# Graph attention, linear attention and an expert FFN on one core: the fills between gathers are replaced by a wait of each gather for the one before

## The reference, cut to what matters

```python
xn = layernorm(x)
f  = xn @ W_n                                  # (N, 8 heads, 32)
el, er = f . attn_l, f . attn_r                # (N, 8, 4) each
e  = ((el[src] + er[dst] + edge16 . attn_m) * edge4).sum(4) / 3.0
e  = where(e > 0, e, 0.2 * e)                  # (E, 8)
a  = softmax of e over the edges of each dst
gnn = segment_sum(f[src] * a, dst)             # (N, 256)
mix = linear attention over all nodes, then layernorm * gamma
x  = x + gnn + mix
x  = x + sum over 8 experts of w_e * FFN_e(layernorm(x))
```

## Time and profile before

| | us |
|---|---|
| median of 2 runs | 3389.78 (3389.61 to 3389.95) |
| the profiled execution | 3383.94 |
| its span in the trace | 3382.3 |
| GpSimd busy | 2077.2 |
| VectorE busy | 2641.9 |
| TensorE busy | 2979.6 |

### The profile page before, as it was taken

One profiled execution on the slowest core, in us unless ns is written; L12 is line 12 of the kernel. 1 busy time (PEld: TensorE's weight loads), 2 busy tenths in 40 slices (PEclk: granted clock), 3 DMA queues, 4 the chain that ended last, 5 costly groups with the idle time before them and its releaser, 6 DMA issues. The chain is left out here.

```text
span 3382.3 us, 76670 instructions
## 1 busy us (share of the span) xinstructions
PE 2979.6 (88%) x21350; PEld 2402.1 (71%) x21351; DVE 2641.9 (78%) x4924; ACT 1699.5 (50%) x5754; POOL 2077.2 (61%) x3347
## 2 busy tenths in 40 slices
PE   7995648889898888998988889888859999999999
PEld 4564537777676767776766677676648888888899
DVE  4574548889888888988988889888857777777786
ACT  4651216556555555665655566555543433333343
POOL 2888878888888888888888888888500000000000
PEclk9997769999999999999999999999879999999999
DMA  7567876666666666666666666666331000100000
GB/s 270 182 209 242 304 239 198 183 181 193 194 187 184 184 195 191 187 187 196 193 182 182 202 184 191 183 194 188 98 98 42 20 20 23 37 20 17 17 21 10
DMA packets 285469, 509.70 MB, mean 151 GB/s; under 512 B 84049, under 2 KB 186870, under 8 KB 277508
## 3 DMA queue, kind: packets, MB, share of 16 engines
q0 software_dynamic: 86032, 287.41, 29.8%
q1 hardware_dynamic: 198900, 220.45, 20.6%
q10 hardware_dynamic: 384, 0.00, 0.0%
HBM read 415.38 MB, written 92.29 MB: 150 GB/s over the span
## 5 line engine op out<-in xcount | busy, mean ns | idle before, releaser
L978 POOL DMA_INDIRECT gat<-scratch_table,idx x1376 | 1332.0, 968 | 231.6 <-issue 226.8
L1337 PE MATMUL ps_s<-msg,oh 128*128 128x272 f32 x4000 | 1055.9, 414 | 41.4 <-DVE msg L1183 26.3
L1337 PEld LDWEIGHTS ps_s<-msg,oh 128*128 128x128 f32 x4000 | 758.5, 197 | 198.1 <-ACT tmp L1044 42.1
L1053 ACT ACTIVATE acc<-acc,sc 128x33 f32<-128x33 f32 x2000 | 458.8, 339 | 230.4 <-DVE acc L1171 230.4
L1580 POOL DMA_DIRECT2D out<-y x13 | 9.8, 756 | 899.6 <-DVE y L1794 899.6
L1183 DVE TENSOR_TENSOR msg<-gat,ps_m 128x2048 f32<-128x2048 f32 x250 | 559.2, 2276 | 0.0
L1627 ACT ACTIVATE h<-ps_h,fsh,fsc 128x512 f32<-128x512 f32 (+1 forms) x416 | 290.8, 750 | 508.9 <-PE ps_h L1840 508.9
L1044 ACT ACTIVATE tmp<-ps_s,sc 128x33 f32<-128x33 f32 x2000 | 384.4, 304 | 17.2
L140 POOL MEMSET rest_e<- 128x192 f32 x1376 | 388.3, 282 | 0.7
L1033 ACT CAST oh<-ps_o 128x1024 f32<-128x1024 bf16 x250 | 259.1, 1037 | 143.4 <-PE ps_o L1277 122.4
L1670 DVE CAST h_hi<-h 128x1024 fp32r<-128x1024 f32 (+1 forms) x208 | 137.2, 660 | 201.7 <-ACT h L1627 201.5
(11 more groups left out here) (217 smaller groups left out, 5406.1 us busy)
## 6 DMA issues: line engine op xcount, KB each, us to landing
d16r<-scratch_dst SPq DMA_DIRECT2D x250, 256.0 KB
scratch_ahead<-stage SPq DMA_DIRECT2D x30, 1152.0 KB, 4.8
gat<-scratch_ahead POOLq DMA_DIRECT2D x30, 1152.0 KB
scratch_acc<-acc SPq DMA_DIRECT2D x250, 136.0 KB
gat<-scratch_table,idx POOLq DMA_INDIRECT x1376
edge<-in_edge SPq DMA_DIRECT2D x250, 88.0 KB
scratch_table<-trow POOLq DMA_DIRECT2D x49, 144.0 KB, 4.1
xin<-in_x SPq DMA_DIRECT2D x49, 128.0 KB, 4.4
```

The costliest lines, as they stand in the source:

```text
L978: pool.indirect_dma_start(out=gat[:, s, c, :], out_offset=None, in_=scr["table_rows"], in_offset=bass.IndirectOffsetOnAxis(ap=idx[:, g * C ...
L1053: act.mul(acc[:, new, cols], acc[:, old, cols], sc[:, j, 0, h:h + 1]).then_inc(scaled, 1)
L1337: last = pe.matmul(ps_s[j][:, 0:SUMS], oh[:, s, j, c, :], msg[:, 2 * (s % 2) + j, c, :], start=(c == 0), stop=(c == C - 1), skip_group_che ...
```

## The change

The class `Rests` and its two scratch tiles go, and with them 1616 fills. The class `Turns` comes in its place. Every gather now raises a semaphore (`engine_sem`) when GpSimd has finished it, apart from the semaphore that the transfer itself raises when the rows have landed, and every gather but the first of a stage waits for the semaphore of the gather before it. The semaphores are the same two as before (`made`, `rested`). The direct loads of groups gathered ahead neither wait nor are waited for.

```diff
-class Rests:
-
-
-    def __init__(self, tile, rested, n):
-        self.tile, self.rested, self.n = tile, rested, n
-
-    def after(self, pool, c):
-        if c % REST_AFTER != REST_AFTER - 1:
-            return
-        for _ in range(RESTS):
-            if self.n:
-                pool.wait_ge(self.rested, self.n)
-            pool.memset(self.tile[:, :], 0.0).then_inc(self.rested, 1)
-            self.n += 1
+class Turns:
+
+
+    def __init__(self, done, n):
+        self.done, self.n = done, n
+
+    def before(self, pool):
+        if self.n:
+            pool.wait_ge(self.done, self.n)
+
+    def begun(self):
+        self.n += 1
+        return self.done
...
                 for c in range(C):
+                    turns.before(pool)
                     pool.indirect_dma_start(
-                        out=stage[:, i % 2, c, :], out_offset=None, in_=scr["table_rows"],
+                        engine_sem=turns.begun(), out=stage[:, i % 2, c, :], out_offset=None, in_=scr["table_rows"],
                         in_offset=bass.IndirectOffsetOnAxis(ap=pidx[:, i * C + c:i * C + c + 1], axis=0),
                     ).then_inc(staged[i % 2], 16)
-                    rests.after(pool, c)
...
             def gather(g, c):
                 s = g % GSLOTS
+                turns.before(pool)
                 pool.indirect_dma_start(
-                    out=gat[:, s, c, :], out_offset=None, in_=scr["table_rows"],
+                    engine_sem=turns.begun(), out=gat[:, s, c, :], out_offset=None, in_=scr["table_rows"],
                     in_offset=bass.IndirectOffsetOnAxis(ap=idx[:, g * C + c:g * C + c + 1], axis=0),
                 ).then_inc(gathered[s], 16)
-                rests.after(pool, c)
```

More of the change, by code:

```diff
@@ L48 @@
 EARLY = 18
-REST_AFTER = 1
-RESTS = 1
-REST_WIDTH = 192
 AHEAD = [0, 1] + [8 + i * (G - 8) // (PRE - 2) for i in range(PRE - 2)]
@@ L216, in phase_nodes @@
         stage = sb("stage", [P, 2, C, ROW])
-        rest = sb("rest_n", [P, REST_WIDTH])
         ps_tr = [ps(f"ps_tr{i}", [P, KD, P]) for i in range(2)]
@@ L430, in _ @@
                 pool.wait_ge(table_out[i], 16 * len(range(i, NT, XB)))
-            rests = Rests(rest, made, READY + 1)
+            turns = Turns(made, READY + 1)
             def gather_ahead(i):
@@ L842, in phase_edges @@
         tmp = sb("tmp", [P, 2, H * HW])
-        rest = sb("rest_e", [P, REST_WIDTH])
         ps_z = ps("ps_z", [P, 2 * C * HT])
@@ L972, in _ @@
             pool.wait_ge(idx_in, 16)
-            rests = Rests(rest, rested, 0)
+            turns = Turns(rested, 0)
             def gather(g, c):
                 s = g % GSLOTS
+                turns.before(pool)
                 pool.indirect_dma_start(
-                    out=gat[:, s, c, :], out_offset=None, in_=scr["table_rows"],
+                    engine_sem=turns.begun(), out=gat[:, s, c, :], out_offset=None, in_=scr["table_rows"],
                     in_offset=bass.IndirectOffsetOnAxis(ap=idx[:, g * C + c:g * C + c + 1], axis=0),
                 ).then_inc(gathered[s], 16)
-                rests.after(pool, c)
             def slot_free(g):
```

## The result

| | before | after |
|---|---|---|
| median | 3389.78 us | 3192.26 us (3190.22 to 3194.29, 2 runs) |
| ratio | | 0.9417, 95% interval 0.939 to 0.9445 |
| span of the profiled execution | 3382.3 us | 3192.4 us |

The change made the kernel 197.5 us (5.8%) faster.

A forecast was written before the change was run, and what follows sets the result against it. GpSimd's gathers were taken to bound node and edge stages. Replacing the fill by a wait lengthens the gap from 0.44 to 0.52 us: 1616 x 0.08 = +129 us, giving 3519 us against the median; range 3260 to 3610 us.

The forecast's parts named there:

- The bound: Node and edge stages: GpSimd's gathers hold up their consumers; the edge stage can win at most 173 us.
- That is 0.2 to 0.25 us more. 0.31 + 0.2 to 0.25 = 0.51 to 0.56 us.: Gap before each waiting gather: a direct DMA's 0.31 us after a release, plus 0.2 to 0.25 us for a gather.
- some 0.2 us of the sequencer's preparation is done before the wait ends: Direct DMA waiting for a semaphore: starts 0.31 us after it, against 0.5 us from the sequencer's last instruction.
- The lower bound: Gap before each waiting gather, from below: queued start 0.16 to 0.30 us plus 0.10 to 0.20 for the wait, 0.26 to 0.50.
- 0.27 to 0.40: Rival on the gap between gathers, in us: cheap wait or early semaphore makes the kernel faster, 3176 to 3228 us; chance 0.28.
- no DMA row starts in under 0.3 us: Sign held against the faster rival: no DMA in the earlier trace starts sooner than 0.3 us after a release.
- the forecast: Gap between gathers of 0.48 to 0.60 us, likeliest 0.52, against 0.44 before: +129 us; chance 0.46.
- Its low end: Faster rival's shortest gap between gathers: 41 us less in the node stage, 173 in the edge stage, 3176 us total.
- lie beside a running gather, as before: GpSimd's sequencer: loads of table entries and waits for free slots run beside a gather of 0.95 us.
- If the gap is under about 0.31 us GpSimd begins to wait for free slots, TensorE's wait for the count goes away, and the scans run at 14.4 us: Edge-stage sign: at so short a gap between gathers, VectorE's own pace would set the scans throughout.
- my slower cases: Gap between gathers over 0.48 us: the forecast at 0.52 (3519 us, chance 0.46), or about 0.80 (3972 us, chance 0.04).

The follow-up runs named there:

- The test by itself: GpSimd alone, output only a copy of x, twelve each of gathers, fills and direct loads, queued or waiting: gathers start 0.30 us after the one ahead either way.

## Why the prediction was wrong, point by point

**The bound: right.** GpSimd's gathers set the pace in both stages, and the edge stage could win 173 us at most. It won 171.7, and then VectorE bounds.

**The step that failed: "That is 0.2 to 0.25 us more. 0.31 + 0.2 to 0.25 = 0.51 to 0.56 us."** The 0.31 us from VectorE's end to a direct DMA already was the whole price of a release. The 0.75 against 0.5 us of the earlier trace rows is counted from the sequencer's instruction: it contains preparation that runs before the wait ends where the wait hangs on the gather itself, and I added a part of it a second time. (The two rows have one of their times to 0.1 us only, and 0.5 us is counted from a move and not from a wait, so the "0.2 to 0.25" was soft besides.) The test by itself is ScalarE's copy: 0.27 us later a gather starts, 0.29 to 0.30 us later a direct load, so a gather pays nothing more. I had written that sentence about direct DMAs ("some 0.2 us of the sequencer's preparation is done before the wait ends") and did not carry it over to the gather. The measured gap is 0.30 us, and not 0.52; 0.75 to 0.77 us appears only where the sequencer itself waits, on a nop or for a slot.

**The lower bound was built on the wrong sum too.** "A queued gather at 0.16 to 0.30 plus 0.10 to 0.20": a wait adds nothing to a queued start of 0.30 us, since GpSimd alone shows 0.30 us with the wait and without it. The row with the right value stood there: a gather queued behind a GpSimd DMA, 0.30 us. The 0.16 us of the earlier trace rows is what is left when a fill covers the rest; a shorter fill leaves 0.19. Of what a fill takes, 0.27 us, 0.14 is therefore shadow, and the fills cost not 0.28 but 0.14 us a gather.

**The weight.** The rival "0.27 to 0.40" described what happened, to the sign that I took for and against it: "no DMA row starts in under 0.3 us" was said against it, and is exactly 0.30. It had a chance of 0.28 against 0.46 for the forecast. Its low end, 41 + 173 = 214 us, took the fall at 0.27 us. At the measured 0.30 the node stage should have won 240 x 0.14 = 33.6 us; it won 21.0 up to the first scan.

**The node stage, missed in all cases.** At a change of the slot the gather waits first for the store, in the sequencer, and starts 0.75 us after the gather ahead (158.45 in the timeline above). A fill used to cover this too: in the kernel before all those starts read 0.16. 28 such places x (0.75 - 0.30) = 12.6 us given back. That 33.6 - 12.6 = 21.0 meets the measured number exactly is partly luck: a few other gaps of up to 4.9 us cost about 7 us more than those of before, while the gathers' own time was 5.4 us shorter (238.6 to 233.2) and the first gather began 1.7 us earlier (96.7 to 95.0), and these nearly cancel. I had said that the sequencer's loads and waits "lie beside a running gather, as before"; in the edge stage they do.

**The signs that I named.** "If the gap is under about 0.31 us GpSimd begins to wait for free slots, TensorE's wait for the count goes away, and the scans run at 14.4 us": all three came (17.4 us in 21 places, 108.1 to 2.5 us, 14.38 us). The gather itself changed little: 955 for 968 ns in the mean, 1376 x 13 ns = 18 us that nobody waits for. The FFN stage kept its length within 3 us.

**What no case held:** that an engine off the path could slow others by being faster. On the chips of the experiments a shorter pitch costs more than it brings. The changed kernel is slower there, as I had forecast, but not for my reason: the gap was 0.30 us there too, and my slower cases had other mechanisms, none of which occurred.

## What to carry over

Split a delay into what runs before a wait ends and what runs behind it, and add only the second; a row "from the sequencer's instruction" and a row "from the semaphore" must not be summed. A filler instruction costs its length less what it hides, and it may hide waits elsewhere (here 28 of them). When a change makes a helper engine's stream denser, profile the others too, on more than one chip: the same edit was worth 6% in the recorded comparison and cost 7 to 9% on three chips afterwards.

## Of the hardware, not expected

- GpSimd started a DMA 0.27 to 0.31 us after the end of what released it, gather or direct, own or foreign semaphore, where the wait hung on the DMA itself; a queued gather has the same 0.30 us, a queued direct load none.
- On four chips, with gathers of 128 rows at a pitch of 1.25 to 1.39 us, what waits for TensorE stood still in pauses (4653 us against 3192 us at 1.25, 4274 against 3390 at 1.39); at 1.60 us this was nearly gone, and with direct loads at 0.94 us there was none.
